# Another order of the items in three hand-written queue plans of an attention and expert kernel

## The chip, the cores and the metric

The kernel runs on one core of a Trainium2 chip. The metric is device time in microseconds of one launch. The engines are PE (matrix products; PEld is its loading of weights), DVE (elementwise work and reductions), ACT (activations and copies with a scale), POOL (elementwise work on SBUF alone) and SP (issues the DMAs). Each engine takes its own list of instructions in order; they wait for each other by semaphores.

## The reference, cut to what matters

Eight batches of 224 queries (512 wide) attend over 750 context rows with 8 heads of 64; then every token passes through all 8 experts of a gated feed-forward layer.

```python
x = x + tanh(g_xattn[0]) * xattn(layernorm(x), ctx, Wq, Wk, Wv, Wo, bo)
x = x + tanh(g_ffn[0]) * ffn(layernorm(x), gate_w, gate_b, rms_w, w1, b1, w2, b2)

def xattn(x, context, Wq, Wk, Wv, Wo, bo):
    q, k, v = heads(x @ Wq), heads(context @ Wk), heads(context @ Wv)
    attn = softmax(einsum("bihd,bjhd->bhij", q, k) * 64 ** -0.5)
    return einsum("bhij,bjhd->bihd", attn, v).reshape(B, N, 512) @ Wo + bo

def ffn(x, ...):
    h = gelu(einsum("nd,edh->neh", x, w1) + b1)
    y = einsum("neh,ehd->ned", h, w2) + b2
    return (y * norm_g[:, None, None]).sum(axis=1)
```

## The kernel before, in words

The kernel has an attention part (batch by batch) and an expert part (two halves of the tokens, 8 experts, four steps each). All products are made of float32r terms: an operand is split into a rounded high part and the rest, and three products (or two) are summed in PSUM. Therefore nearly every item on PE is drained twice: ACT writes the high part (function `hi`), then DVE the low part (`drain`).

The order of the attention part is not left to a scheduler. It is written out as three plans, each with one list for PE, ACT, DVE and POOL: `HEAD_PLAN` (what comes ahead of the first batch's heads), `BODY_PLAN` (one batch; the first batch leaves out its items of the batch before, the six middle batches are a loop) and `END_PLAN` (the last batch, with the first step of the experts woven in). Each engine walks its list, and `make` (PE), `hi` (ACT), `drain` and `special` (DVE) and `handle` (POOL) issue what an item needs of that engine, behind its semaphore waits. In an item, `>` means the next batch and `<` the batch before. The letters:

- `C` context columns split into parts (half, pair), `N` a piece of a weight matrix split, `X` the normalised queries transposed, `L` and `A` layer-norm statistics and their application, `Y` the same transposition for the expert part (drained by ACT alone).
- `K` keys (group, pair of heads, half: 12 matmuls), `Q` queries (group, pair: 12), `V` values (group, tile of 125 rows: 12).
- `S` scores of a head and half of the queries on PE (4 matmuls), their maximum on DVE, their exponential on ACT; `R` one over the row sum (DVE); `M` the scaling of the probabilities (half 0 on ACT, half 1 on POOL; in the last batch ACT does both from head 4 on).
- `T` two of six blocks of the probabilities transposed (head, third: 4 transpositions; the first third waits for both `M`), `P` the product with the values (6), `D` the sum of its terms (DVE, then POOL after each odd head), `O` the output projection (12, added to the residual by DVE).
- In the last plan `G`, `U`, `W`, `F`, `Z`, `B`, `H` are the experts' inputs, their split, the first weights, constants and the first step's seven products `H0` to `H6`.

What ties the order together is four PSUM banks. The items `X K Q V T O Y P B H` take them in turn in the order of PE's list (function `banks`), so each such item on PE first waits until the item four places earlier among these has been drained: by DVE's low part, for `Y` by ACT's copy:

```python
if before is not None:
    pe.wait_ge(lo_out[before[0]], number(before, b))
```

Scores have two places of their own: `S` waits for the exponential of the same half of the head before. The exponential of head h waits until PE has transposed all of head h-2, whose buffer it takes. `P` waits for the last `V` of its group, then for each third of its `T`. `K` of one half waits, per pair of context columns, for that pair's low part:

```python
for c in range(KC):
    pe.wait_ge(lo_out["C"], number(("C", db, half, c // 2), b))
```

SP's list (loads of context, x and weights, stores of both scratch tensors) is written separately and waits by the same semaphores.

## Time and profile before

| what | value |
|---|---|
| runs | 1819.58, 1821.06, 1828.24 us (median 1821.06) |
| span of the profiled execution | 1816.1 us, 31801 instructions, granted clock 1.000 |
| PE | 1794.9 us busy (99%), 9720 matmuls |
| PEld | 1615.8 us (89%) |
| DVE | 1330.5 us (73%) |
| ACT | 810.9 us (45%) |
| POOL | 1184.1 us (65%) |

The profiled execution's span is 5.0 us under the median of the runs. Busy time of PE is drawn from the start of each matmul to a modelled end, so neighbours overlap in the rows; the distance between two items is read from their starts. The attention part ends near 648 us; the first key projection begins at 8.03 us, the first batch near 35, the six middle batches lie between 106 and 573 us, 77.7 us each. The rest is the expert part.

### The profile page before, as it was taken

The page shows a single profiled execution, that of the slowest core. Times are in us where ns is not written, and L with a number is a line of the kernel's source. Part 1 is how long each engine was busy: PE and PEld are TensorE (multiplying, and loading weights), DVE is VectorE, ACT ScalarE, POOL GpSimd, SP SyncE. Part 2 cuts the span into 40 slices and gives each one's busy share as a digit, 9 for nine tenths or more (in the row PEclk, how much of TensorE's full clock was granted, in tenths as well). Part 3 has the DMA queues.
Part 4 walks back from the last instruction along what each step waited for, and adds up shares of the span by engine and source line. Part 5 has one row for each costly group of instructions (what it writes and reads, how often), then busy time and mean ns, then how long its engine had stood idle before and what let it go on. Part 6 is the DMA issues. An engine that isn't in the chain of part 4 may idle for free.

```text
span 1816.1 us, 31801 instructions
## 1 busy us (share of the span) xinstructions
PE 1794.9 (99%) x9720; PEld 1615.8 (89%) x9720; DVE 1330.5 (73%) x2308; ACT 810.9 (45%) x1574; POOL 1184.1 (65%) x900
## 2 busy tenths in 40 slices
...
GB/s 176 39 41 36 57 22 61 21 62 40 34 69 16 92 97 74 66 54 62 58 58 58 58 58 58 47 66 106 127 57 63 52 69 47 69 46 69 46 47 53
DMA packets 52057, 110.35 MB, mean 61 GB/s; under 512 B 13208, under 2 KB 25496, under 8 KB 52000
## 3 DMA queue, kind: packets, MB, share of 16 engines
...
q14 instruction: 27, 0.22, 0.0%
...
## 4 chain that ended last, share of the span: by engine, by line
PE 96%; DVE 1%; issue 1%; ACT 1%; DMA 0%; SPq 0%; POOL 0%; ACTq 0%; DVEq 0%
PE bank L781 33%; PE scores L754 28%; PE bank L625 19%; PE scores L696 5%; PE bank L706 4%; PE bank L718 4%; PE bank L632 1%; PE scores L839 0%; DVE h_sum L1051 0%; DMA ctx_raw<-in_ctx 0%; ACT hs L1318 0%; PE bank L754 0%; ACT probs L1190 0%; DVE xs L900 0%; ACT h_full L1317 0%
## 5 line engine op out<-in xcount | busy, mean ns | idle before, releaser
L781 PE MATMUL bank<-w2s,hs 128*128 128x512 f32 x2688 | 620.9, 389 | 1.3 <-DVE xres L1018 1.0
L781 PEld LDWEIGHTS bank<-w2s,hs 128*128 128x128 f32 x2688 | 504.4, 188 | 105.1 <-issue 1.5
L754 PE MATMUL scores<-xs,w1s 128*128 128x448 f32 x2646 | 549.5, 366 | 3.6 <-DVE h_sum L1051 3.5
L754 PEld LDWEIGHTS scores<-xs,w1s 128*128 128x128 f32 x2646 | 495.8, 188 | 48.7 <-DVE h_sum L1051 3.8
L1051 DVE TENSOR_TENSOR h_sum<-scores,h_sum 128x448 f32<-128x448 f32 x441 | 262.7, 619 | 183.3 <-PE scores L754 182.8
L1317 ACT ACTIVATE h_full<-h_sum,b1T 128x448 f32<-128x448 f32 x256 | 170.9, 668 | 303.1 <-DVE h_sum L1051 292.4
L1066 DVE TENSOR_TENSOR acc<-bank,acc 128x512 f32<-128x512 f32 x337 | 229.1, 686 | 71.5 <-PE bank L781 62.9
L900 DVE TENSOR_TENSOR hs<-h_full,hs 128x448 fp32r<-128x448 f32 x256 | 237.9, 930 | 52.2 <-ACT hs L1318 52.1
L1190 ACT ACTIVATE h_sum<-scores 128x448 f32<-128x448 f32 x63 | 34.3, 545 | 475.4 <-PE scores L754 475.4
L1391 POOL TENSOR_SCALAR probs<-probs,row_inv 112x750 f32<-112x750 f32 x60 | 130.6, 2176 | 100.1 <-DVE row_inv L989 100.1
L1493 POOL CAST w1s<-w_stage 128x768 fp32r<-128x768 f32 x64 | 69.0, 1078 | 168.5 <-PE scores L754 168.5
L1318 ACT ACTIVATE hs<-h_sum,b1T 128x448 fp32r<-128x448 f32 x256 | 167.7, 655 | 0.0
L1521 POOL TENSOR_TENSOR w2s<-w_stage,w2s 128x1024 fp32r<-128x1024 f32 x64 | 155.1, 2423 | 11.5 <-POOL w2s L1518 11.5
L1507 POOL TENSOR_TENSOR w1s<-w_stage,w1s 128x1024 fp32r<-128x1024 f32 x64 | 155.0, 2422 | 11.3 <-POOL w1s L1504 11.3
L625 PE MATMUL bank<-ctxT,wk 128*128 128x376 f32 (+1 forms) x768 | 147.0, 341 | 8.0 <-DVE ctxT L900 8.0
L625 PE MATMUL bank<-wv,ctxT 128*125 128x256 f32 x1152 | 152.1, 283 | 0.0
L625 PEld LDWEIGHTS bank<-wv,ctxT 128*125 128x125 f32 x1152 | 142.6, 186 | 1.0
L625 PEld LDWEIGHTS bank<-ctxT,wk 128*128 128x128 f32 x768 | 131.5, 191 | 10.4 <-issue 9.4
L1498 POOL TENSOR_TENSOR w1s<-w_stage,w1s 128x768 fp32r<-128x768 f32 x64 | 137.8, 2153 | 0.0
L1234 ACT ACTIVATE probs<-scores,neg_max 112x750 f32<-112x750 f32 x128 | 113.3, 886 | 32.1 <-DVE neg_max L983 20.8
L900 DVE TENSOR_TENSOR probsT<-bank,probsT 125x448 fp32r<-125x448 f32 x192 | 115.9, 618 | 12.7 <-ACT probsT L1190 11.1
L1190 ACT ACTIVATE probsT<-bank 125x448 fp32r<-125x448 f32 x192 | 100.0, 542 | 49.3 <-PE bank L706 49.0
(128 smaller groups left out, 2197.3 us busy)
## 6 DMA issues: line engine op xcount, KB each, us to landing
w_stage<-in_L_ffn_w SPq DMA_DIRECT2D x128, 512.0 KB, 3.5
...
xa<-in_x SPq DMA_DIRECT2D x16, 224.0 KB, 2.7
xres<-in_x SPq DMA_DIRECT2D x16, 224.0 KB, 2.7
x_scratch<-xres SPq DMA_DIRECT2D x16, 224.0 KB, 2.3
xt_scratch<-yT SPq DMA_DIRECT2D x16, 224.0 KB, 2.8
...
```

Source lines behind the costliest of these rows:

```text
L625: mm = pe.matmul(bank, s[i], m[j], start=first and n == 0, stop=last and n == total - 1)
L754: mm = pe.matmul(product_bank(g, name)[:, 0:TH], w1s[j % 2][:, s, W_OF[name], kc, :], xs[:, i, m, kc, :], start=n == 0, stop=n == 5)
L781: mm = pe.matmul(bank[:, :], hs[j % 2][:, s, ht, t * P:(t + 1) * P], w2s[j % 2][:, m, ht, :], start=n == 0, stop=n == 5)
L900: return dve.tensor_tensor(out, a_, b_.bitcast(F32), ALU.subtract)
L1051: dve.tensor_tensor(h_sum[:, q, :], product_bank(g, product)[:, 0:TH], h_sum[:, other, :], ALU.add).then_inc(sum_out, 1)
L1066: dve.tensor_tensor(home, ps[(3 * j + t) % RING][:, :], b2_sum[:, :] if first else home, ALU.add).then_inc(y_added, 1)
L1190: return act.activation(dst, src, ACT.Copy, scale=scale)
L1317: act.activation(h_full[:, q, :], src, ACT.Gelu, bias=bias)
L1318: act.activation(hs[j % 2][:, 0, ht, half * TH:(half + 1) * TH], src, ACT.Gelu, bias=bias).then_inc(h_act, 1)
L1498: pool.tensor_tensor(w[:, 1, 0:3], raw[:, 1:4], w[:, 0, 0:3].bitcast(F32), ALU.subtract).then_inc(w1_split, 1)
L1507: pool.tensor_tensor(w[:, 1, 3:7], raw[:, 4:8], w[:, 0, 3:7].bitcast(F32), ALU.subtract).then_inc(w1_split, 1)
L1521: pool.tensor_tensor(w[:, 1], w2_stage[:, :, :], w[:, 0].bitcast(F32), ALU.subtract).then_inc(w2_split, 1)
```

## The change

All three plans get new lists for all four engines. Each list holds the same items as before, in another order; the functions that issue them, the DMAs' list and all sizes stay. The lists of the last plan for ACT and POOL are left out here; in POOL's, `G0 G1 G2` now stand ahead of `W0.0`, and `G3` ahead of `W0.2`.

```diff
 HEAD_PLAN = {
     "pe": plan("""
-        K0.0.0 X0 X1 K0.1.0 Q0.0 Q0.1 K0.0.1 V0.0 V0.1 S0.0 S0.1 K0.1.1 S1.0 V0.2 V0.3 V0.4 S1.1 V0.5
+        K0.0.0 X0 X1 K0.1.0 Q0.0 Q0.1 K0.0.1 V0.0 V0.1 V0.2 S0.0 S0.1 K0.1.1 V0.3 S1.0 S1.1 V0.4 V0.5
     """),
     "act": plan("""
-        N0 C0.0 C0.1 N1 K0.0.0 C1.0 X0 N2 X1 C1.1 K0.1.0 Q0.0 Q0.1 K0.0.1 V0.0 S0.0 V0.1 K0.1.1 S0.1 V0.2 V0.3
-        S1.0 V0.4 S1.1 V0.5 M0.0
+        N0 C0.0 C0.1 N1 K0.0.0 C1.0 X0 X1 K0.1.0 C1.1 N2 Q0.0 Q0.1 K0.0.1 V0.0 V0.1 S0.0 V0.2 K0.1.1 S0.1 S1.0
+        V0.3 V0.4 M0.0 V0.5 S1.1
     """),
     "dve": plan("""
-        N0 C0.0 C0.1 L0.0 L0.1 A0.0 A0.1 K0.0.0 X0 N1 X1 C1.0 K0.1.0 C1.1 N2 Q0.0 K0.0.1 Q0.1 S0.0 R0.0 V0.0
-        S0.1 K0.1.1 V0.1 V0.2 S1.0 V0.3 R0.1 V0.4 S1.1 V0.5
+        N0 C0.0 L0.0 L0.1 C0.1 A0.0 A0.1 N1 K0.0.0 X0 X1 K0.1.0 C1.0 C1.1 N2 Q0.0 Q0.1 K0.0.1 S0.0 V0.0 S0.1
+        V0.1 V0.2 K0.1.1 R0.0 R0.1 S1.0 V0.3 V0.4 S1.1 V0.5
     """),
     "pool": plan("""
-        L0.0 L0.1 N3 N4 N5 N6 M0.1 N7
+        L0.0 L0.1 N3 N4 N5 M0.1 N6 N7
     """),
 }
 BODY_PLAN = {
     "pe": plan("""
-        K1.0.0 S2.0 S2.1 T0.0 T0.1 T0.2 O<0 K1.1.0 P0 S3.0 T1.0 T1.1 K1.0.1 S3.1 Q1.0 O<1 T1.2 V1.0 Y<0 K1.1.1
-        P1 T2.0 Y<1 S4.0 T2.1 S4.1 T2.2 V1.1 Q1.1 V1.2 V1.3 P2 S5.0 T3.0 S5.1 T3.1 T3.2 V1.4 P3 V1.5 V>0.0 S6.0
-        T4.0 T4.1 T4.2 V>0.1 S6.1 V>0.2 X>0 X>1 P4 S7.0 T5.0 T5.1 Q>0.0 K>0.0.0 T5.2 K>0.1.0 S7.1 K>0.0.1 V>0.3
-        P5 T6.0 V>0.4 S>0.0 S>0.1 T6.1 T6.2 Q>0.1 P6 T7.0 K>0.1.1 V>0.5 T7.1 T7.2 S>1.0 S>1.1 P7
+        K1.0.0 S2.0 T0.0 T0.1 S2.1 T0.2 K1.1.0 O<0 S3.0 P0 T1.0 K1.0.1 T1.1 S3.1 Q1.0 O<1 Y<0 T1.2 V1.0 K1.1.1
+        P1 Y<1 T2.0 S4.0 T2.1 S4.1 T2.2 V1.1 V1.2 Q1.1 S5.0 V1.3 P2 T3.0 T3.1 S5.1 T3.2 V1.4 V1.5 S6.0 P3
+        V>0.0 T4.0 T4.1 T4.2 V>0.1 S6.1 V>0.2 X>0 X>1 P4 T5.0 T5.1 S7.0 Q>0.0 K>0.0.0 K>0.1.0 T5.2 S7.1
+        K>0.0.1 V>0.3 P5 T6.0 S>0.0 S>0.1 V>0.4 T6.1 T6.2 Q>0.1 P6 T7.0 K>0.1.1 V>0.5 T7.1 S>1.0 T7.2 S>1.1 P7
     """),
     "act": plan("""
-        K1.0.0 T0.0 M1.0 T0.1 T0.2 S2.0 K1.1.0 P0 S2.1 T1.0 M2.0 T1.1 K1.0.1 Q1.0 S3.0 T1.2 V1.0 S3.1 Y<0 K1.1.1
-        P1 T2.0 Y<1 T2.1 T2.2 S4.0 M3.0 S4.1 V1.1 Q1.1 V1.2 V1.3 M4.0 P2 T3.0 T3.1 T3.2 P3 S5.0 V1.4 M5.0 V1.5
-        V>0.0 S5.1 T4.0 S6.0 V>0.1 T4.1 T4.2 X>0 V>0.2 X>1 M6.0 P4 T5.0 S6.1 T5.1 Q>0.0 T5.2 K>0.0.0 S7.0
-        K>0.1.0 S7.1 K>0.0.1 M7.0 P5 V>0.3 T6.0 V>0.4 T6.1 T6.2 S>0.0 Q>0.1 T7.0 M>0.0 P6 S>0.1 K>0.1.1 T7.1
-        V>0.5 T7.2 P7 S>1.0 S>1.1
+        K1.0.0 T0.0 T0.1 S2.0 T0.2 M1.0 K1.1.0 S2.1 P0 T1.0 T1.1 K1.0.1 Q1.0 S3.0 T1.2 Y<0 V1.0 M2.0 K1.1.1
+        S3.1 P1 T2.0 T2.1 Y<1 V1.1 S4.0 T2.2 S4.1 V1.2 M3.0 Q1.1 P2 V1.3 T3.0 T3.1 T3.2 S5.0 V1.4 V1.5 M4.0 P3
+        S5.1 V>0.0 M5.0 T4.0 S6.0 V>0.1 T4.1 T4.2 X>0 V>0.2 X>1 P4 T5.0 Q>0.0 S6.1 T5.1 K>0.0.0 K>0.1.0 T5.2
+        S7.0 S7.1 K>0.0.1 M6.0 P5 M7.0 V>0.3 T6.0 V>0.4 T6.1 T6.2 S>0.0 S>0.1 Q>0.1 T7.0 M>0.0 P6 K>0.1.1 T7.1
+        V>0.5 T7.2 S>1.0 P7 S>1.1
     """),
     "dve": plan("""
-        D<7 R1.0 R1.1 K1.0.0 T0.0 S2.0 T0.1 O<0 T0.2 S2.1 K1.1.0 D0 R2.0 S3.0 T1.0 L<1.0 T1.1 R2.1 S3.1 A<1.0
-        K1.0.1 Q1.0 O<1 L<1.1 T1.2 V1.0 A<1.1 K1.1.1 R3.0 D1 T2.0 S4.0 S4.1 R3.1 T2.1 T2.2 R4.0 V1.1 L>0.0 Q1.1
-        V1.2 V1.3 D2 T3.0 L>0.1 T3.1 T3.2 R4.1 S5.0 S5.1 R5.0 V1.4 D3 A>0.0 V1.5 V>0.0 S6.0 A>0.1 R5.1 T4.0
-        V>0.1 T4.1 R6.0 T4.2 X>0 V>0.2 X>1 S6.1 D4 T5.0 T5.1 Q>0.0 R6.1 T5.2 S7.0 K>0.0.0 S7.1 R7.0 K>0.1.0
-        K>0.0.1 D5 T6.0 R7.1 V>0.3 S>0.0 V>0.4 T6.1 T6.2 S>0.1 R>0.0 Q>0.1 T7.0 D6 K>0.1.1 T7.1 V>0.5 T7.2 R>0.1
-        S>1.0 S>1.1
+        R1.0 D<7 K1.0.0 R1.1 S2.0 T0.0 T0.1 S2.1 T0.2 K1.1.0 O<0 D0 T1.0 R2.0 R2.1 L<1.0 S3.0 A<1.0 K1.0.1
+        T1.1 Q1.0 O<1 L<1.1 A<1.1 T1.2 V1.0 R3.0 S3.1 K1.1.1 D1 T2.0 S4.0 R3.1 S4.1 T2.1 V1.1 R4.0 T2.2 L>0.0
+        R4.1 V1.2 Q1.1 V1.3 D2 T3.0 S5.0 T3.1 A>0.0 T3.2 L>0.1 V1.4 R5.0 S5.1 V1.5 D3 V>0.0 S6.0 R5.1 T4.0
+        A>0.1 T4.1 R6.0 V>0.1 T4.2 X>0 V>0.2 S6.1 X>1 T5.0 D4 S7.0 T5.1 Q>0.0 R6.1 K>0.0.0 S7.1 T5.2 K>0.1.0
+        R7.0 K>0.0.1 D5 S>0.0 V>0.3 R7.1 S>0.1 T6.0 V>0.4 T6.1 T6.2 R>0.0 Q>0.1 D6 T7.0 K>0.1.1 V>0.5 T7.1
+        T7.2 R>0.1 S>1.0 S>1.1
     """),
     "pool": plan("""
-        D<7 M1.1 L<1.0 L<1.1 M2.1 D1 M3.1 C>0.0 C>0.1 L>0.0 L>0.1 M4.1 D3 M5.1 C>1.0 C>1.1 M6.1 D5 M7.1 M>0.1
+        D<7 M1.1 L<1.0 L<1.1 M2.1 D1 M3.1 L>0.0 M4.1 C>0.0 C>0.1 L>0.1 M5.1 D3 C>1.0 C>1.1 M6.1 M7.1 D5 M>0.1
     """),
 }
 END_PLAN = {
     "pe": plan("""
-        K1.0.0 S2.0 T0.0 S2.1 T0.1 T0.2 O<0 O<1 P0 T1.0 Q1.0 Q1.1 S3.0 Y<0 K1.1.0 K1.0.1 T1.1 T1.2 K1.1.1 S3.1
-        P1 S4.0 T2.0 T2.1 V1.0 T2.2 V1.1 S4.1 V1.2 S5.0 P2 T3.0 T3.1 T3.2 S5.1 V1.3 V1.4 P3 S6.0 V1.5 S6.1 T4.0
-        Y<1 T4.1 T4.2 P4 S7.0 T5.0 T5.1 T5.2 S7.1 P5 B0 T6.0 T6.1 T6.2 H0 P6 H1 H2 T7.0 T7.1 T7.2 H3 P7 H4 H5 H6
-        O0 O1
+        K1.0.0 S2.0 T0.0 S2.1 T0.1 O<0 T0.2 O<1 P0 Q1.0 T1.0 S3.0 Q1.1 K1.1.0 Y<0 K1.0.1 T1.1 T1.2 K1.1.1 S3.1
+        P1 S4.0 T2.0 T2.1 S4.1 T2.2 V1.0 V1.1 S5.0 V1.2 S5.1 P2 T3.0 V1.3 T3.1 T3.2 V1.4 P3 S6.0 Y<1 V1.5 T4.0
+        S6.1 T4.1 T4.2 P4 T5.0 T5.1 T5.2 S7.0 S7.1 B0 P5 T6.0 T6.1 T6.2 P6 H0 H1 H2 T7.0 T7.1 T7.2 H3 P7 H4 H5
+        H6 O0 O1
     """),
...
     "dve": plan("""
-        R1.0 D<7 K1.0.0 T0.0 S2.0 S2.1 T0.1 T0.2 O<0 R1.1 O<1 L<1.0 L<1.1 T1.0 D0 R2.0 A<1.0 Q1.0 S3.0 Q1.1
-        K1.1.0 R2.1 A<1.1 K1.0.1 T1.1 T1.2 S3.1 R3.0 H0 K1.1.1 D1 T2.0 S4.0 T2.1 R3.1 R4.0 V1.0 S4.1 T2.2 V1.1
-        R4.1 V1.2 D2 S5.0 T3.0 T3.1 T3.2 S5.1 R5.0 S6.0 V1.3 V1.4 R5.1 D3 V1.5 T4.0 U0 T4.1 T4.2 S6.1 U1 R6.0
-        S7.0 R6.1 D4 T5.0 T5.1 T5.2 S7.1 D5 R7.0 B0 T6.0 T6.1 T6.2 U2 U3 U4 R7.1 D6 H1 H2 U5 T7.0 T7.1 T7.2 U6
-        H3 D7 H4 H5 H6 O0 O1 L1.0 L1.1 A1.0 A1.1
+        D<7 S2.0 R1.0 K1.0.0 T0.0 O<0 R1.1 S2.1 T0.1 T0.2 O<1 L<1.0 L<1.1 D0 A<1.0 T1.0 Q1.0 Q1.1 K1.1.0 A<1.1
+        R2.0 S3.0 T1.1 K1.0.1 R2.1 T1.2 S3.1 K1.1.1 D1 R3.0 T2.0 T2.1 R3.1 H0 S4.0 S4.1 V1.0 R4.0 R4.1 V1.1
+        T2.2 S5.0 V1.2 D2 S5.1 T3.0 T3.1 V1.3 T3.2 R5.0 D3 V1.4 R5.1 S6.0 T4.0 T4.1 T4.2 V1.5 S6.1 U0 U1 R6.0
+        R6.1 D4 T5.0 T5.1 S7.0 T5.2 B0 S7.1 R7.0 T6.0 D5 T6.1 T6.2 U2 U3 U4 R7.1 D6 H1 H2 U5 T7.0 T7.1 T7.2 U6
+        D7 H3 H4 H5 H6 O0 O1 L1.0 L1.1 A1.0 A1.1
     """),
...
```

## Rows read from the trace of the kernel before

**Rows 1.** Table of stretches: length, busy time (instructions) per engine, clock, DMA.

```profile
107.00:573.00 466.00, 465.58 (x3216) 447.69 (x3215) 382.33 (x817) 326.41 (x720) 217.40 (x181) 1.00 0.15 43
...
612.00:650.00 38.00, 33.85 (x179) 27.11 (x178) 34.04 (x59) 30.46 (x54) 28.09 (x24) 1.00 0.13 42
```

**Rows 2.** Timeline of PE, one middle batch: start, length, engine, line, operation.

```profile
363.16 1.38 PE L718 MATMUL bank<-probsT,values 125*128 125x448 f32 x6
364.62 0.66 PE L706 MATMUL bank<-ident,probs 112*125 112x112 f32 x4
...
366.54 0.92 PE L696 MATMUL scores<-keys,queries 128*112 128x376 f32 x4
...
367.65 1.66 PE L625 MATMUL bank<-wv,ctxT 128*125 128x256 f32 x12
369.15 1.49 PE L625 MATMUL bank<-xnT,wq 128*128 128x224 f32 x12
...
373.32 1.38 PE L718 MATMUL bank<-probsT,values 125*128 125x448 f32 x6
374.54 0.85 PE L696 MATMUL scores<-keys,queries 128*112 128x376 f32 x4
375.23 0.59 PE L706 MATMUL bank<-ident,probs 112*125 112x112 f32 x4
...
407.17 1.58 PE L625 MATMUL bank<-xnT,wq 128*128 128x224 f32 x12
...
412.31 1.59 PE L625 MATMUL bank<-wv,ctxT 128*125 128x256 f32 x12
```

**Rows 3.** Timeline of POOL in the same batch: the scaling M2.1.

```profile
362.29 2.18 POOL L1391 TENSOR_SCALAR probs<-probs,row_inv 112x750 f32<-112x750 f32 x1
```

**Rows 4.** Timeline of ACT in the same batch: T2.0, Y<1, T2.1, S4.0, M3.0, Q1.1, V1.3.

```profile
365.31 0.54 ACT L1190 ACTIVATE probsT<-bank 125x448 fp32r<-125x448 f32 x1 [0.38 <-PE bank L706]
365.75 0.54 ACT L1190 ACTIVATE yT<-bank 128x448 f32<-128x448 f32 x1
366.81 0.55 ACT L1190 ACTIVATE probsT<-bank 125x448 fp32r<-125x448 f32 x1 [0.52 <-PE bank L706]
...
368.36 0.88 ACT L1234 ACTIVATE probs<-scores,neg_max 112x750 f32<-112x750 f32 x1
...
369.22 0.92 ACT L1190 ACTIVATE probs<-probs,row_inv 112x750 f32<-112x750 f32 x1
...
371.15 1.44 ACT L1190 ACTIVATE queries<-bank 64x224 fp32r<-64x224 f32 x4
...
373.52 0.39 ACT L1190 ACTIVATE values<-bank 125x256 fp32r<-125x256 f32 x1 [0.52 <-PE bank L625]
```

**Rows 5.** Timeline of DVE in the same batch: Q1.1's low parts.

```profile
372.80 1.60 DVE L964 SCALAR_TENSOR_TENSOR queries<-bank,queries 64x224 fp32r<-64x224 f32 x4
```

**Rows 6.** Timeline of SP at the start: both loads of x issued.

```profile
2.32 0.95 SPq L456 DMA_DIRECT2D xa<-in_x  x2
```

**Rows 7.** DMA issues of the first 40 us: KB each, median us to landing.

```profile
xa<-in_x SPq DMA_DIRECT2D x2, 224.0 KB, 6.6
```

**Rows 8.** Timeline of DVE in the head: C0.1 and A0.0 (L0.0 and L0.1 between).

```profile
8.88 0.94 DVE L900 TENSOR_TENSOR ctxT<-ctx_raw,ctxT 128x752 fp32r<-128x752 f32 x1 [1.00 <-ACT ctxT L1190]
...
11.98 0.54 DVE L896 TENSOR_SCALAR xa<-xa,mean_var,rstd 112x512 f32<-112x512 f32 x1
```

**Rows 9.** Timeline of PE in the head: K0.0.0, K0.1.0, Q0.0.

```profile
8.03 4.10 PE L625 MATMUL bank<-ctxT,wk 128*128 128x376 f32 x12 [8.03 <-DVE ctxT L900]
...
13.95 2.31 PE L625 MATMUL bank<-ctxT,wk 128*128 128x376 f32 x12
17.13 1.12 PE L625 MATMUL bank<-xnT,wq 128*128 128x224 f32 x8 [0.86 <-DVE xnT L900]
```

**Rows 10.** Timelines of PE (P4) and DVE (U0) in the last batch.

```profile
618.80 1.21 PE L718 MATMUL bank<-probsT,values 125*128 125x448 f32 x4 [0.98 <-DVE probsT L900]
...
616.94 1.27 DVE L900 TENSOR_TENSOR xs<-x_raw,xs 128x896 fp32r<-128x896 f32 x1
```

12 lines of the change are left out of this document (6 added, 6 removed).

## The prediction

> **What bounds the kernel now.** I read the granted clock and span first (one core, 1816.1 us, clock 1.000), then the table of stretches, then who waits on PE, then the timeline of each engine in one middle batch. The table of stretches says that PE is the bound everywhere: in the six middle batches (107 to 573 us) it is busy 465.58 of 466.00 us, while DVE is busy 382.33 and ACT 326.41 [rows 1]. So an order can win only what PE still waits. Its visible idle time is 21.2 us in all, and 8.0 of that is the start, before the first key projection has its operands. The last batch is the one attention stage with much of it: 38.00 - 33.85 = 4.15 us between 612 and 650 [rows 1]. The two passes of experts after that are outside the three plans, and I move nothing there.
>
> The busy share of PE hides short waits, because a matmul that waits a tenth of a microsecond is simply drawn longer or later. I therefore read the distance from the start of one item to the start of the next. There are few such waits in a middle batch: P1 needs 364.62 - 363.16 = 1.46 us where P2 needs 374.54 - 373.32 = 1.22 [rows 2], because T2.0 behind it waits for the scaling M2.1, which POOL ends at 362.29 + 2.18 = 364.47 [rows 3]. T2.0 itself is then drawn 0.07 longer than its neighbours. That is 0.3 us per middle batch, nearly all that a better body order could give back.
>
> **The change, part by part.** Nothing is added or removed: the same items stand in each list, in another order. So the PE work stays, and each term is a wait that goes or comes. I went through the new lists queue by queue, put each item at the later of two times (its engine free, its input ready), and took durations and handovers from rows.
>
> *Body, gain.* O<1 keeps its place but Q1.0 is drained earlier on DVE (S3.1's maximum now comes after it), and PE reaches T2.0 0.3 us later behind Y<1. By the rows M2.1 ends about 0.5 us ahead of T2.0 then. The wait of 0.3 us goes: -0.3.
>
> *Body, first new wait: V1.1.* Four PSUM banks go round, so V1.1 takes the bank of Y<1 and waits for ACT's copy of it. PE now issues Y<1 before T2.0, but ACT's list has T2.0 T2.1 Y<1 V1.1. ACT can copy T2.1 only 366.81 - 366.54 = 0.27 us after PE starts S4.1; 0.55 for that copy and 0.54 for Y<1, less 0.10 of overlap, make 1.26 us [rows 2, 4]. The handover from ACT to PE isn't seen alone; it is not below 0, and the nearest row has 0.15 (M2.1's end to T2.0's start [rows 2, 3]). PE wants V1.1 367.65 - 366.54 = 1.11 us after S4.1's start [rows 2]. Cost 0.15 to 0.30; I take 0.25, nearer to the one handover that is seen.
>
> *Second: T3.1.* It takes the bank of Q1.1, which DVE must have finished. ACT now holds S4.0 T2.2 S4.1 V1.2 M3.0 behind V1.1, and Q1.1 behind them. From V1.1's end on PE: 0.20 until ACT starts, then 0.39 + 0.88 + 0.54 + 0.88 + 0.39 + 0.92 + 1.44 [rows 4], less about 0.45 of overlap between neighbours, is 5.2 us; DVE's four operations on Q1.1 add 1.60 [rows 5]: 6.8, and the handover, 0 to 0.15. PE reaches T3.1 after Q1.1, two V, P2, S5.0 (375.23 - 369.15 = 6.08 [rows 2]) and T3.0 (0.4): 6.5. Cost 0.30 to 0.45; I take 0.40. Before, ACT did T2.2, both exponentials and M3.0 while PE was still on V1.1, and PE did Q1.1 right behind it.
>
> *Third: V>0.5.* It takes the bank of Q>0.1. ACT now does S>0.1 ahead of Q>0.1. From the end of T6.2 on PE: 0.27 + 0.55 for T6.2, 0.88 + 0.88 for S>0.0 and S>0.1, 1.44 for Q>0.1, less 0.25 of overlap, then 1.60 on DVE: 5.4, and the handover. PE does Q>0.1 P6 T7.0 K>0.1.1 in 412.31 - 407.17 = 5.14 us [rows 2], the same four in both orders. Cost 0.3 to 0.5; I take 0.40.
>
> *Fourth and fifth:* X>1 behind DVE's T4.2 (DVE now does V>0.1 between T4.1 and T4.2) and Q>0.1 behind T6.0 (DVE has S>0.1 ahead of T6.0). By the same durations PE comes 0.05 to 0.25 and 0 to 0.15 us too early; I take 0.15 and 0.05, an estimate.
>
> Sum per middle batch: 0.25 + 0.40 + 0.40 + 0.15 + 0.05 - 0.30 = +0.95; with the lower ends 0.50, with the upper ones 1.35. Six batches: +5.7 (3.0 to 8.1). The first batch has no Y<, no O< and no M2.1 wait: the other four, +1.0 (0.65 to 1.35).
>
> *Moves that I cost at nothing.* T items between others instead of in runs: S4.1 and T2.2, each behind the other kind, take 367.65 - 366.54 = 1.11 together; an S behind a P takes 375.23 - 374.54 = 0.69 [rows 2] and a T within a run some 0.42 (an estimate), which is the same. POOL's M4.1, M5.1, M7.1 and M0.1 ahead of copies and D items: each ends 2 us or more before its T; what is put back, D3 (some 4 us with its two additions), must be ready when DVE reaches D4, and stays 0.7 us ahead; without that cover D4, and with it P5's bank, would be late by the difference. SP's list is unchanged. The stores and loads that wait for O<0 (now some 2 us later) are used 40 us later.
>
> *Head.* DVE now does L0.0 and L0.1 before C0.1. Both need the rows of x, issued from 2.32 us on [rows 6] with 6.6 us to landing [rows 7], so L0.0 starts at 8.9. The two take 11.98 - 8.88 - 0.94 = 2.2 us [rows 8], so C0.1 ends near 12.0 instead of 9.8. K0.0.0 has its first six matmuls from 8.03 and needs C0.1 for the other six: PE stands from about 10.2 to 12.1. Against that N1 is split earlier, so that Q0.0, which now starts at 17.13 after 0.86 us of waiting for X1 [rows 9], waits on X1 alone. Those twelve matmuls took 4.10 us, the next of the same shape 2.31 [rows 9]; 376 columns at the slower spacing (0.31) are the 1.2 GHz level, though the table prints the clock as 1.00 there. If the clock rises at 13.2 as now, K0.0.0 ends at 13.6, X1 is ready 0.5 later than now, and C1.0, C1.1 and N2, which DVE does after X1 now, hold nothing more: +0.5. If the rise comes later by the hole (1.9 us), X1 is 0.9 late, and K0.1.0, C1.0, C1.1, N2, Q0.0, Q0.1, K0.0.1 follow on DVE one behind the other: S0.0 is 1.2 late; if the rise starts afresh with the second half of K0.0.0, 2.1. I take +1.2. The Trainium skill (TensorE: Matmul & The Clock Gate, Part 1) says that the array is throttled by default and that activity releases it; by that a hole delays the rise, which speaks for the upper end, 2.1 instead of 1.2.
>
> *Last batch.* DVE no longer does U0 (1.27 us) between T4.0 and T4.1 [rows 10], which kept P4 waiting (the visible part is 0.98 us [rows 10]). But the new list puts V1.5 behind T4.2, P4 waits for V1.5 first, and P4 now follows T4.2 directly: 0.27 until ACT starts, T4.2's copy (0.55), and, as estimates from the sizes, 0.6 for its subtraction and 0.4 for V1.5's on DVE end some 1.9 us after PE is there. The wait changes its cause and hardly its size. H0 no longer fills PE between T6.2 and P6, so P6 waits 1.4 us for D5 and T6.2, and the same work follows: O0 starts as long after the batch's beginning as now. I take 0 (-2 to +2).
>
> Total: 5.7 + 1.0 + 1.2 + 0 = +7.9 us. The profiled execution goes from 1816.1 to 1824.0; the median of the runs is 5.0 above its span (1821.06), so 1829.0. By the bounds alone, 3.0 + 0.65 + 0.5 - 2 to 8.1 + 1.35 + 2.1 + 2: 1823.2 to 1834.6.
>
> **The rivals.**
>
> *The orders do what they say (not slower).* If the five waits don't show, say because a bank is given back 0.3 us earlier than I add up, the body gives -0.3 x 6, the head and the last batch's 4.15 us can give some 3: -5, 1816. It decides at spacings of 0.4 us, and the rows behind the second and third are sums of seven durations. For it: DVE has 18% of idle time in the body. Against it: ACT's and DVE's queues go in order, and those sums are longer than PE's.
>
> *DVE falls behind (clearly slower).* ACT's list has Q>0.0 S6.1 T5.1 and DVE's T5.1 Q>0.0, so DVE stands for 1.44 + 0.88 + 0.55 us after PE's Q>0.0. Following DVE from there (T5.1 Q>0.0 K>0.0.0 S7.1 T5.2 K>0.1.0) I get K>0.1.0's bank free 8.7 us after Q>0.0's end, and P5 wants it after 8.73. There is no margin; every further 0.1 us late costs 0.1 in each of seven batches. With 0.7 per batch: +4.9, 1834.
>
> *Nothing happens:* gains and waits cancel, 1821 +-1.
>
> *PE's own busy time shrinks.* The Trainium skill (Perfetto Trace Analysis, Identifying the Most-Contended Engine) holds that busy matmul time is a bad measure and that weight loads show the room. As a mechanism here: weight loads cover 447.69 of 466.00 us in the body [rows 1], so 18.3 us would be open to better neighbours: 1803. But the items with short loads (O, P) run at the spacing of their columns, which no order shortens.
>
> **How the numbers follow.** Forecast 0.55, orders work 0.20, DVE behind 0.14, nothing 0.09, shrinking 0.02. The forecast's own range is 1823.2 to 1834.6; to leave out no more than 2 in 10 I go to 1817 and 1836. What a measurement can tell from no change is about 0.5%, 9.1 us: slower than 1830.2 are the DVE case and about 0.22 of the forecast: 0.36. Faster than 1812 are the last case and a little of the second: 0.04. The rest, 0.60, is within.
>
> **What would show it.** Middle batches of 78.7 instead of 77.7 us; on PE a late start of V1.1, T3.1 and V>0.5 in each, less so of X>1; P1 back at 1.22; in the head a hole after six matmuls and a later first S; in the last batch P4 waiting for V1.5. I am wrong if the middle batches keep 77.7 or less, or if one new wait is over 0.6 us.

## The result and the profile after

The changed kernel takes 1842.61 us (median of 4 runs) against 1823.61 for the kernel before beside it (4 runs): ratio 1.0117, 95% interval 1.0092 to 1.0142. It is slower, as forecast, but outside the forecast range of 1817 to 1836. The span of the profiled execution is 1840.9 us, 24.8 more than before, three times the +7.9 of the forecast. Read from the starts of the items on PE, it is made of:

| stage | before | after | forecast | measured |
|---|---|---|---|---|
| head, to the first K1.0.0 | 35.26 | 37.65 | +1.2 | +2.39 |
| first batch | 71.12 | 73.70 | +1.0 | +2.58 |
| six middle batches | 466.35 | 479.86 | +5.7 | +13.51 |
| last batch, to the end of O1 | 75.39 | 77.89 | 0 | +2.50 |
| expert part | 1167.96 | 1171.81 | 0 | +3.85 |

A middle batch takes 80.0 us instead of 77.7 (forecast: 78.7). The table of stretches of the changed kernel (columns as in [rows 1]; six middle batches but for their edges, then 38 us of the last batch as in [rows 1]):

```profile
112.00:591.00 479.00, 475.52 (x3214) 447.54 (x3212) 380.19 (x816) 327.01 (x720) 216.76 (x181) 1.00 0.15 42
631.00:669.00 38.00, 33.48 (x180) 27.15 (x178) 32.06 (x55) 31.05 (x55) 26.53 (x25) 1.00 0.10 35
```

PE now visibly stands 3.5 us in the body, where it stood 0.4 [rows 1]; the other 10 us of the loss are drawn as longer or later matmuls. The waits on PE in the page of the changed kernel name what is new (engine, line, who was waited for: us in total, times, longest):

```profile
PE bank L625 <- DVE ctxT L900: 10.5, 3, 8.0
PE scores L754 <- DVE h_sum L1051: 5.5, 7, 2.0
PE bank L718 <- DVE keys L900: 2.1, 7, 0.4
PE bank L718 <- DVE values L900: 1.9, 1, 1.9
PE bank L718 <- DVE att_sum L1010: 1.3, 1, 1.3
PE bank L706 <- DVE queries L964: 1.0, 6, 0.3
...
PE bank L625 <- DVE keys L900: 0.4, 1, 0.4
```

The first is the head (8.0 at the start as before, then 2.1 and 0.4), the third P5 in seven batches, the fourth and fifth P4 and P6 of the last batch, the sixth T3.1 in six batches, the last V1.0 of the first batch. The second lies in the expert part, whose code is the same.

In a middle batch (the fifth of the eight) the items answering to [rows 2] are, on PE of the changed kernel, T3.0, T3.1, V>0.3, P5, T6.1 with T6.2, and Q>0.1:

```profile
387.31 0.59 PE L706 MATMUL bank<-ident,probs 112*125 112x112 f32 x4
388.05 0.69 PE L706 MATMUL bank<-ident,probs 112*125 112x112 f32 x4 [0.16 <-DVE queries L964]
...
413.39 1.58 PE L625 MATMUL bank<-wv,ctxT 128*125 128x256 f32 x12
415.26 1.49 PE L718 MATMUL bank<-probsT,values 125*128 125x448 f32 x6 [0.29 <-DVE keys L900]
...
419.80 1.02 PE L706 MATMUL bank<-ident,probs 112*125 112x112 f32 x8
420.91 1.60 PE L625 MATMUL bank<-xnT,wq 128*128 128x224 f32 x12
```

T3.1 starts 0.74 behind T3.0, where T items in a run follow after some 0.4: this is the forecast wait. P5 starts 1.87 behind V>0.3, whose matmuls need 1.42: this was only a rival in the prediction. In the kernel before, V>0.3, P5, and T6.1 with T6.2 (Q>0.1 follows at 407.17 [rows 2]):

```profile
400.50 1.58 PE L625 MATMUL bank<-wv,ctxT 128*125 128x256 f32 x12
401.92 1.39 PE L718 MATMUL bank<-probsT,values 125*128 125x448 f32 x6
...
406.37 1.02 PE L706 MATMUL bank<-ident,probs 112*125 112x112 f32 x8
```

There P5 follows 1.42 behind V>0.3, and Q>0.1 0.80 behind T6.1; in the changed kernel the latter is 1.11.

### The profile page after: what moved, and what is told of

It is laid out like the page before. It is cut to its first block, busy times and chain, and to the rows that moved or that the text cites. A ratio compares the mean times of both kernels' runs of the same rounds, so it can differ in the third digit from the quotient of the medians.

```text
span 1840.9 us, 31795 instructions
## 1 busy us (share of the span) xinstructions
PE 1810.7 (98%) x9720; PEld 1618.2 (88%) x9720; DVE 1331.3 (72%) x2308; ACT 812.0 (44%) x1574; POOL 1184.7 (64%) x900
## 3 DMA queue, kind: packets, MB, share of 16 engines
q1 hardware_dynamic: 52000, 109.64, 19.4%
## 4 chain that ended last, share of the span: by engine, by line
PE 75%; issue 10%; DVE 8%; ACT 4%; POOL 2%; DMA 0%; DVEq 0%; ACTq 0%; SPq 0%; POOLq 0%
PE bank L781 33%; PE scores L754 28%; PE bank L625 8%; PE bank L718 2%; PE bank L706 2%; DVE neg_max L983 2%; PE scores L696 2%; ACT probs L1234 1%; DVE probsT L900 1%; DVE queries L964 1%; DVE keys L900 1%; ACT queries L1190 1%; POOL probs L1391 1%; DVE h_sum L1051 1%; PE bank L632 0%
## 5 line engine op out<-in xcount | busy, mean ns | idle before, releaser
L983 DVE TENSOR_REDUCE neg_max<-scores 112x1 f32<-112x750 f32 x128 | 117.9, 927 | 2.4 <-PE scores L696 1.6
```

The costliest lines, as they stand in the source:

```text
L983: dve.tensor_reduce(neg_max[0:QT, i:i + 1], ps_scores[qt][0:QT, SCORES], AX.X, ALU.max, negate=True).then_inc(max_out, 1)
```

## The experiments

Item times below are distances between starts on PE. Lists are BODY_PLAN's unless another is named; of a list, only the items around a move are shown. A ratio is that to the kernel before, timed beside the run, with its 95% interval.

**Each plan alone.** Three kernels: the kernel before with one of the three new plans.

> The kernel before with the new HEAD_PLAN alone. Theory A (the loss of the head is the hole in PE behind the first six matmuls of K0.0.0, which DVE's later C0.1 causes, together with the slow first matmuls behind it): the first K1.0.0 starts 2.4 us later than before (35.3 to 37.7), the rest of the kernel keeps its distances, +2.4 us in all (about 1826). Rival B (by the prediction's working the hole costs 1.2; the other 1.2 us seen in the changed kernel belong to the body's lists, which take over K, V and S items in another order): +1.2 at the first K1.0.0, and the first batch keeps its 71.1 us.

> The kernel before with the new BODY_PLAN alone. Theory A (the loss is made of waits inside a batch): each middle batch takes 80.0 us instead of 77.7, the first batch 2.6 us more, so +16 us in all. Rival B (the lists of the three plans were found together, and part of the loss or gain lies at the seams to head and last batch): the middle batches still take 80.0, but the first or the last batch differ by over 1 us from what they take in the changed kernel (73.7 for the first). The prediction's working gives 78.7 for a middle batch and +6.7 in all.

> The kernel before with the new END_PLAN alone. Theory A (P4 behind V1.5 and P6 behind T6.2 in the last batch cost what they show, and nothing hides it): the last batch takes 2.5 us more than before, and the expert part keeps its length. Rival B (the prediction's working): P4's wait only changes its cause, the last batch keeps its length within 0.5. Rival C (the 3.8 us by which the expert part of the changed kernel is longer come from this plan's order of weights, loads and last items on POOL and DVE): the last batch +2.5 and the expert part +3.8, +6.3 in all.

These are the three parts of the diff ahead of the prediction. Measured: only_head 1822.88 us, ratio 1.0015 (1.0005 to 1.0025), first K1.0.0 at 36.89, first batch 71.0; only_body 1836.55, ratio 1.0087 (1.0070 to 1.0104), middle batches 80.0, first batch 73.73, last batch 75.64; only_end 1822.81, ratio 1.0013 (1.0003 to 1.0022), last batch 77.87. Each plan keeps its loss without the others, and the three ratios' excess over 1 (0.0015, 0.0087 and 0.0013) makes 0.0115 of the 0.0117 measured for all: the losses add and do not lie at the seams. The head's +1.6 lies between the two expectations. Of rival C for only_end: its profiled execution does have the expert part 3.7 longer, but only_body, with the old END_PLAN, has 2.5, and end_two_moves below, with the same list on POOL, has none. That difference has another cause (gate_later).

**ACT's T5.1 ahead of Q>0.0,** in the changed kernel:

```diff
-T5.0 Q>0.0 S6.1 T5.1 K>0.0.0
+T5.0 T5.1 Q>0.0 S6.1 K>0.0.0
```

> The changed kernel with one item moved in ACT's body list: T5.1 goes from behind S6.1 to ahead of Q>0.0, where DVE's list has it. Theory A (DVE stands 2.6 us for T5.1 behind Q>0.0 and S6.1 on ACT, falls behind, and gives the bank of K>0.1.0 back 0.55 us too late for P5, and by that Q>0.1 0.3 too late): P5 and Q>0.1 start without a wait, each middle batch takes about 79.2 instead of 80.0, -6 us in all. Rival B (DVE catches its idle time up before K>0.1.0, and P5 waits for ACT or for D items that share POOL): the middle batch stays within 0.2 of 80.0.

Measured: 1836.56 us against 1842.61 (ratios 1.0089, 1.0072 to 1.0106, and 1.0117); all six middle batches take 79.2, the number of theory A. On DVE, T5.1 and behind it Q>0.0 to K>0.1.0 in the changed kernel:

```profile
408.98 0.62 DVE L900 TENSOR_TENSOR probsT<-bank,probsT 125x448 fp32r<-125x448 f32 x1 [2.63 <-ACT probsT L1190]
409.52 1.59 DVE L964 SCALAR_TENSOR_TENSOR queries<-bank,queries 64x224 fp32r<-64x224 f32 x4
411.14 0.16 DVE L989 RECIPROCAL row_inv<-row_sum 112x1 f32<-112x1 f32 x1
411.34 1.11 DVE L900 TENSOR_TENSOR keys<-bank,keys 64x376 fp32r<-64x376 f32 x2
412.48 0.94 DVE L983 TENSOR_REDUCE neg_max<-scores 112x1 f32<-112x750 f32 x1
413.45 0.62 DVE L900 TENSOR_TENSOR probsT<-bank,probsT 125x448 fp32r<-125x448 f32 x1
414.10 1.11 DVE L900 TENSOR_TENSOR keys<-bank,keys 64x376 fp32r<-64x376 f32 x2
```

and with T5.1 moved, on PE, V>0.3, P5, T6.1 with T6.2, and Q>0.1:

```profile
410.21 1.58 PE L625 MATMUL bank<-wv,ctxT 128*125 128x256 f32 x12
411.62 1.39 PE L718 MATMUL bank<-probsT,values 125*128 125x448 f32 x6
...
416.06 1.02 PE L706 MATMUL bank<-ident,probs 112*125 112x112 f32 x8
417.17 1.60 PE L625 MATMUL bank<-xnT,wq 128*128 128x224 f32 x12
```

DVE stood 2.63 us for T5.1 and did 6 us of work behind it without a pause. Moved, P5 follows 1.41 behind V>0.3, without a wait, and the waits of the items ahead of it (S7.1, K>0.0.1) go too: 0.8 in all. But Q>0.1 still starts 1.11 behind T6.1, as in the changed kernel, so my guess that its 0.3 came from the late P5 was wrong: that 79.2 came out all the same was luck, since P5 and the items ahead of it gave 0.8 where I had 0.55. The last batch was 78.75 here, 0.9 longer, since PE's granted clock fell to 0.50 after its wait at P4 (row of this kernel's table of stretches):

```profile
636.00:638.00 2.00, 2.00 (x10) 1.99 (x9) 1.47 (x6) 1.76 (x5) 2.00 (x3) 0.50 0.00 0
```

**Three more moves on ACT, then three on DVE.** To the move above act_moves adds, on ACT, Q1.1 ahead of M3.0, S>0.1 behind Q>0.1 and Y<1 ahead of T2.0; act_dve_moves adds to these, on DVE:

```diff
-V1.0 R3.0 S3.1 K1.1.1 D1
+V1.0 R3.0 K1.1.1 S3.1 D1
-T4.1 R6.0 V>0.1 T4.2 X>0
+T4.1 R6.0 T4.2 V>0.1 X>0
-D5 S>0.0 V>0.3 R7.1 S>0.1 T6.0
+D5 T6.0 S>0.0 V>0.3 R7.1 S>0.1
```

> The changed kernel with four items moved in ACT's body list, each to where the wait that the prediction named would go: T5.1 ahead of Q>0.0 (alone it gave 0.8 per batch), Q1.1 ahead of M3.0 (T3.1), S>0.1 behind Q>0.1 (V>0.5), Y<1 ahead of T2.0 (V1.1). Theory A (each wait is the one ACT item in front): in a middle batch T3.1's wait of 0.4 and V1.1's of 0.2 go and V>0.5 loses its 0.1, so the batch takes 78.5 instead of the 79.2 with T5.1 alone. Rival B (the waits have a second cause close behind, DVE's queue, so that one move gives back little): not under 78.9.

> The same four moves on ACT and three on DVE: K1.1.1 ahead of S3.1 (bank of T2.1), T6.0 right behind D5 (bank of Q>0.1), V>0.1 behind T4.2 (bank of X>1). Theory A (Q>0.1's 0.32 is the maximum of S>0.1 ahead of T6.0 on DVE, the fifth term of the prediction at a wrong size, T2.1's 0.32 the maximum of S3.1 ahead of K1.1.1): both go and X>1's 0.2 too, the middle batch takes 77.7 or less, the same as before the change or 0.2 under it by the gain at M2.1, and the whole kernel is about 5 us over the kernel before, by its head and last batch. Rival B (Q>0.1 and T2.1 wait for something else, Q>0.1 for the late D5, T2.1 for A<1.1 that DVE does at half speed while POOL scales): 78.2 or more.

Measured: act_moves 1833.33 us, ratio 1.0063 (1.0039 to 1.0086), middle batches 78.95. T3.1's wait went (-0.40), but V1.4, three items later, came 0.27 later, and V1.1's 0.2 fell by 0.12 only. This is rival B's size. act_dve_moves 1852.56, ratio 1.0165 (1.0137 to 1.0192), middle batches 81.1 (one 83.1, in which the granted clock fell to 0.50 for some 3 us): the theory's 77.7 failed. The time lies within rival B's "78.2 or more", but not for its reason, since the moves did cause what they should (X>1's 0.17 and Q>0.1's 0.31 went, and T2.1 follows 0.76 behind S4.0 instead of 0.96) and made larger waits beside it. S4.1, which needs the exponential of S3.1, came 1.23 later, T2.2 behind it 0.48, and T6.1 0.88. On ACT of act_dve_moves, the exponential of S3.1, then P1 and Y<1; on DVE of the same, K1.1.1 and the maximum of S3.1:

```profile
385.88 0.89 ACT L1234 ACTIVATE probs<-scores,neg_max 112x750 f32<-112x750 f32 x1 [2.22 <-DVE neg_max L983]
...
386.88 0.35 ACT L1190 ACTIVATE att_tmp<-bank 64x224 f32<-64x224 f32 x1
387.25 0.54 ACT L1190 ACTIVATE yT<-bank 128x448 f32<-128x448 f32 x1
```

```profile
383.69 1.10 DVE L900 TENSOR_TENSOR keys<-bank,keys 64x374 fp32r<-64x374 f32 x2 [0.29 <-ACT keys L1190]
384.82 0.94 DVE L983 TENSOR_REDUCE neg_max<-scores 112x1 f32<-112x750 f32 x1
```

The maximum came 1.5 us later, and ACT stood for it 2.22 us with P1, Y<1, T2.0 and T2.1 queued behind; PE's S4.1 then stood 1.10 us for the exponential. A move on one in-order list lands on the other one.

**The head.** The kernel before with the new HEAD_PLAN and one move, then two, on DVE:

```diff
-N0 C0.0 L0.0 L0.1 C0.1 A0.0
+N0 C0.0 C0.1 L0.0 L0.1 A0.0
-X0 X1 K0.1.0 C1.0 C1.1 N2
+X0 X1 C1.0 K0.1.0 C1.1 N2
```

> The kernel before with the new HEAD_PLAN, and in it DVE's C0.1 again ahead of L0.0 and L0.1, nothing else. Theory A (hole and slow first matmuls behind it are the whole loss of the head): no hole behind the sixth matmul of K0.0.0, the faster spacing is there from about 13 us on as before, and the first K1.0.0 starts at 35.3 or earlier. Rival B (the other moves of the head cost too: V0.1, S1.0 and Q0.1 wait for drains that now come one behind the other on DVE): about 36.1.

> The kernel before with the new HEAD_PLAN, and on DVE C0.1 again ahead of L0.0 and C1.0 again ahead of K0.1.0. With C0.1 alone put back the hole in K0.0.0 went, but the first K1.0.0 stayed at 37.1, since K0.0.1 stood 0.75 us for the low parts of C1.0 and C1.1. Theory A (the step of the prediction that these hold nothing more was wrong, and they cost about 1 us of the head): K0.0.1 starts without its wait, S0.0 comes 0.7 to 1.0 us earlier behind Q0.0 than with C0.1 alone, the first K1.0.0 near 36.2. Rival B (what is left of the head's loss is the time at which the faster spacing comes, which differs from execution to execution): S0.0 comes as long behind Q0.0 as with C0.1 alone, 10.1 us.

Measured: with C0.1 alone (head_c01) the first K1.0.0 is at 37.11, with both (head_c1) at 35.51; the whole times don't tell either kernel from the one before (ratios 1.0002, 0.9986 to 1.0017, and 0.9997, 0.9985 to 1.0009). The hole (PE's pause) in K0.0.0, on PE of the changed kernel, then, on PE of head_c01, K0.0.0 in one piece and K0.0.1:

```profile
8.01 2.22 PE L625 MATMUL bank<-ctxT,wk 128*128 128x376 f32 x6 [8.01 <-DVE ctxT L900]
12.34 2.25 PE L625 MATMUL bank<-ctxT,wk 128*128 128x376 f32 x6 [2.12 <-DVE ctxT L900]
```

```profile
7.60 4.48 PE L625 MATMUL bank<-ctxT,wk 128*128 128x376 f32 x12 [7.60 <-DVE ctxT L900]
...
21.09 2.31 PE L625 MATMUL bank<-ctxT,wk 128*128 128x374 f32 x12 [0.59 <-DVE ctxT L900]
```

With the hole gone K0.0.1 still stood for C1.0, which DVE did behind K0.1.0, and DVE had waited 1.95 us for K0.1.0 with C1.0 ready. From Q0.0 to S0.0 it takes 10.11 in head_c01 and 9.10 in head_c1: theory A of head_c1 holds (1.0). In head_c01 neither theory A (35.3 or earlier) nor rival B (36.1) does. The other 0.6 between the two are the faster spacing: the granted clock rose at 12.2 us in head_c1 and at 17.1 in head_c01. From Q0.0 to the first K1.0.0, where the clock is up, it takes 18.1 in all ten profiled executions with the old list, 19.2 to 19.4 in the five with the new one, 19.4 in head_c01 and 18.4 in head_c1.

**The last batch.** Four kernels. end_two_moves (new END_PLAN; PE's H0 again between T6.2 and P6, DVE's V1.5 ahead of T4.0), end_h3 (new END_PLAN; DVE's H3 again ahead of D7), m61_pool (the kernel before; M6.1 on POOL behind D3), end_u6 (new END_PLAN; ACT's U6 again ahead of T7.0):

```diff
-T6.2 P6 H0 H1
+T6.2 H0 P6 H1
-T4.0 T4.1 T4.2 V1.5 S6.1
+V1.5 T4.0 T4.1 T4.2 S6.1
...
-U6 D7 H3 H4
+U6 H3 D7 H4
...
-T5.2 S7.0 M6.1 U2
+T5.2 S7.0 U2
-W0.2 D3 W0.3
+W0.2 D3 M6.1 W0.3
...
-H0 M7.0 M7.1 T7.0 U6 T7.1 T7.2
+H0 M7.0 M7.1 U6 T7.0 T7.1 T7.2
```

> The kernel before with the new END_PLAN, and in it H0 again between T6.2 and P6 on PE, and DVE's V1.5 ahead of T4.0 instead of behind T4.2. Theory A (the waits of P4 and P6 make most of the last batch's loss): P6's wait of 1.4 goes, P4's falls from 2.0 to about 1.5, and the last batch takes 76.0 instead of 77.9. Rival B (as in the prediction's working, filling PE there only moves the wait to the products H behind it, since the same work follows): 77.4 or more.

> The kernel before, with the scaling M6.1 of the last batch on POOL behind D3 instead of on ACT, the plans otherwise as before. Theory A (from 40 to 62 us of the last batch ACT stands idle for 0.4 us and sets the pace, so that 0.9 us less on ACT makes all behind it earlier): T7.0 and the end of the last batch come about 0.9 us earlier, 74.5 instead of 75.4 us. Rival B (PE's waits on DVE at P4, P5 and P6 set the pace, as the prediction had it): the last batch stays within 0.3 of 75.4 or gets longer, since POOL scales in 2.2 us.

> The kernel before with the new END_PLAN, and in it DVE's H3 again ahead of D7. Theory A (0.7 us of the last batch's loss is H6 on PE waiting for the bank of H3, which DVE drains only behind D7, and D7 waits for ACT's P7): the wait of 0.7 between H5 and H6 goes, the last batch takes 77.2 instead of 77.9; the rest, the 1.5 us that ACT stands idle longer, stays. Rival B (DVE's sums H5 and H6 behind set the end of the batch, whatever stands ahead of them): 77.8 or more.

> The kernel before with the new END_PLAN, and on ACT U6 again ahead of T7.0. In the new list ACT stands 0.84 us for T7.0 behind M7.1 and does U6 only then; in the list before U6 filled that wait. Theory A (at its end the last batch is paced by ACT and the chain M7.1, T7.2, H2, P7 on ACT, D7 on DVE and POOL, O0 on PE): T7.2, P7, D7 and O0 come 0.85 earlier, the last batch takes 77.0 instead of 77.9. Rival B (PE's waits at P4, P5 and P6 or DVE's sums set the end): within 0.3 of 77.9.

Measured, last batch: end_two_moves 77.92 against 77.87 for only_end. P4 started 1.34 earlier, but H0 in P6's place stood as long as P6 had (1.27 us in the rows), now itself behind D5 for the bank of P5, and T7.0 stood 1.09 us for ACT's scaling instead of 0.38, so that it starts 63.4 us into the batch as in only_end: rival B. end_h3 (79.0, one execution) is not clear: H6's 0.68 went, but O0 behind it came 0.77 later, since D7 was late then, and 1.07 were lost at P4 to the lower clock. m61_pool 78.62, 3.2 worse, as rival B allows, and theory A fails before it is tested: on PE the product H0 came at 633.31, when POOL ended the low half of its weights at 633.20 (in this execution the batch starts 2.1 us later than in the kernel before):

```profile
627.79 1.04 POOL L1504 CAST w1s<-w_stage 128x1024 fp32r<-128x1024 f32 x1
628.80 2.10 POOL L1473 TENSOR_TENSOR x_mix<-x_raw,x_mix 128x896 f32<-128x896 f32 x1
630.84 2.36 POOL L1507 TENSOR_TENSOR w1s<-w_stage,w1s 128x1024 fp32r<-128x1024 f32 x1
```

In the kernel before these weights end at 628.84 and H0 starts at 628.95 (the profile puts H0's wait down to DVE's copy for B0, which ends 0.12 ahead of the weights), and POOL stands 0.7 us in all from 605.7 to 629.9: POOL paces H0, and there is hardly room on it. In the batch H0 comes 2.2 later, the length of the scaling. Some of the 3.2 is again a clock of 0.50 for 3 us behind that pause. end_u6 77.09: theory A (0.8 of 0.85). On ACT of only_end, M7.0 with M7.1, T7.0 and U6, then, on ACT of end_u6, the same work without the pause:

```profile
634.05 1.72 ACT L1190 ACTIVATE probs<-probs,row_inv 112x750 f32<-112x750 f32 x2
636.61 0.54 ACT L1190 ACTIVATE probsT<-bank 125x448 fp32r<-125x448 f32 x1 [0.84 <-PE bank L706]
637.05 0.94 ACT L1190 ACTIVATE xs<-x_raw 128x896 fp32r<-128x896 f32 x1
```

```profile
634.50 1.72 ACT L1190 ACTIVATE probs<-probs,row_inv 112x750 f32<-112x750 f32 x2
636.12 0.94 ACT L1190 ACTIVATE xs<-x_raw 128x896 fp32r<-128x896 f32 x1
637.06 1.42 ACT L1190 ACTIVATE probsT<-bank 125x448 fp32r<-125x448 f32 x3
```

The whole times show little of this: ratios 1.0013 (0.9998 to 1.0028) for end_two_moves, 1.0020 (1.0009 to 1.0031) for m61_pool, 1.0000 (0.9989 to 1.0011) for end_u6, and a single 1821.92 us for end_h3.

**The gates' small operations behind the third sum,** in the kernel before (the call that issues them, moved from `step` into `sums`):

```diff
                 for name in {1: ("U2",), 2: ("C11",), 3: ("U3",), 4: ("C22", "V"), 5: ("C21",), 6: ("C12",)}.get(i, ()):
                     h_sums(g, name)
+                if i == 3 and g[2] == 3 and isinstance(g[1], int) and g[1] == NE - 1:
+                    gate(g[0], 2)
...
-                    if closing and j == 3 and i == 1:
-                        gate(p, 2)
```

> The kernel before with one move in DVE's expert part and nothing in the three plans: the six small operations on the gates (lines 1146 to 1151) of a pass's last step go from ahead of the third sum to behind it, where DVE stands 2.15 us for ACT anyway. Theory A (the 2.2 or 3.7 us by which the last 300 us are longer in some executions, of both kernels, come from two of these operations being held by a POOL operation that began just ahead of them, 1.04 for 0.17 us and 2.28 for 0.65): the expert part always has its shorter length, executions of the kernel before at 1820 to 1823 no longer occur, and the median is 1818, 2.5 us under that of before. Rival B (the difference comes from something else in the last 300 us, a load or the clock): median within 1 us of before, the same spread.

Measured: 1819.39 us (11 runs, 1818.5 to 1821.4) against 1820.10 (27 runs, 1817.7 to 1826.7), ratio 0.9994 (0.9985 to 1.0004). In the time theory A's number failed and rival B's held: the median is within 1 us of before, and four of the 11 runs lie at 1820 to 1822, where theory A wanted none. The traces do show theory A's mechanism. DVE, POOL and PE in the changed kernel:

```profile
1809.71 1.04 DVE L1148 TENSOR_SCALAR gate_small<-gate_small 128x7 f32<-128x7 f32 x1
1810.79 0.20 DVE L1149 RECIPROCAL gate_small<-gate_small 128x7 f32<-128x7 f32 x1
1811.02 2.28 DVE L1150 TENSOR_TENSOR gate_small<-gate_small 128x7 f32<-128x7 f32 x1
```

```profile
1809.68 1.04 POOL L1518 CAST w2s<-w_stage 128x1024 fp32r<-128x1024 f32 x1 [3.65 <-DMA w_stage<-in_L_ffn_w]
1810.90 2.37 POOL L1521 TENSOR_TENSOR w2s<-w_stage,w2s 128x1024 fp32r<-128x1024 f32 x1 [0.18 <-POOL w2s L1518]
```

```profile
1814.28 4.03 PE L754 MATMUL scores<-xs,w1s 128*128 128x448 f32 x12 [1.97 <-DVE h_sum L1051]
```

Both long operations end 0.03 behind the POOL operation that began ahead of them. In the kernel before POOL's cast begins 0.02 behind the first of the two, which takes 0.17; the second takes 0.65 and ends with that cast. Which starts first is decided by hundredths of a microsecond, between DVE's sum ahead of the gates and the transfer for which the cast waits. In nine of the fourteen profiled executions with the old place both operations are long, PE stands 1.9 to 2.0 us for the third sum, and the expert part is 2.0 to 3.9 us longer; in the other five, and in the three with the new place, PE has no such wait and the part takes 1167.8 to 1168.1. (In the new place one of the operations still takes 1.2 to 1.4 us, but nothing on PE waits for it.) Of the nine, seven lose 2.0 to 2.5. The changed kernel (3.9) and only_end (3.7) lose more, since there the granted clock also fell behind PE's wait; the row of the changed kernel's table of stretches:

```profile
1815.30:1818.60 3.30, 3.30 (x11) 2.85 (x10) 1.70 (x4) 1.96 (x4) 0.00 (x0) 0.50 0.01 2
```

**Versions meant to beat both.** best (three moves on the kernel before) and two_moves (without M6.1). The move in the body, on PE and on ACT:

```diff
-P1 T2.0 Y<1
+P1 Y<1 T2.0
```

> Three moves on the kernel before: the body's Y<1 ahead of T2.0 on PE and on ACT (the only wait that the new body gave back, at M2.1), the scaling M6.1 of the last batch on POOL, and the gates' small operations behind the third sum. Theory A (each gives what the theories say): middle batches of 77.4 instead of 77.7, a last batch of 74.5, the shorter expert part always: about 1815.5, 5 us under before. Rival B (Y<1 ahead of T2.0 only shifts the wait to V1.1, as in the changed kernel): middle batches of 77.7 or more, and only the other two gains, about 1817.

> Two moves on the kernel before: the body's Y<1 ahead of T2.0 on PE and on ACT (it gave 0.25 per middle batch in the run with three moves), and the gates' small operations behind the third sum; M6.1 stays on ACT, since on POOL it cost 3.2 us. Theory A: middle batches of 77.5, the last batch of 75.4 again, the shorter expert part always: 1.5 us under the kernel with the gates' move alone, about 1818, ratio 0.999. Rival B (the last batch's length was lost to its new start, not to M6.1): last batch still over 77, no gain.

Measured: best 1821.31, ratio 1.0005 (0.9995 to 1.0014): middle batches 77.47, but the last batch 79.39 by M6.1. two_moves 1818.00, ratio 0.9982 (0.9971 to 0.9993): middle batches 77.44, the shorter expert part, last batch 76.26 (with 0.81 as the clock between 625 and 630 us). It is faster than the kernel before by some 0.2% and than the changed one by 1.3%.

## Why the prediction was wrong in size

The direction and the way of reading (the distances on PE, each list walked in order) held: the loss is a row of small waits. Their sum was not. The step that failed is the list of waits in the body: +0.95 per middle batch was forecast and 2.25 measured, since the waits for a late bank at P5 (0.84) and at T2.1 (0.31) had no term and Q>0.1's was too small. Of the 16.9 us between forecast and measurement, 7.8 lie in the six middle batches, 1.6 in the first, 1.2 in the head, 2.5 in the last and 3.9 in the expert part.

- *The gain at M2.1* was right: P1 and T2.0 together need 0.37 less (forecast 0.3).
- *V1.1, T3.1 and X>1* were right: 0.20, 0.39 and 0.17 against 0.25, 0.40 and 0.15. *V>0.5* was 0.10 against 0.40. The prediction's own sum (5.4 on ACT and DVE, 5.14 on PE, a handover of up to 0.15) gives 0.2 to 0.4 and not 0.3 to 0.5; the rest fits Q>0.1, whose bank it takes, coming 0.32 late itself.
- *Q>0.1* was mis-sized, 0.32 against 0.05. The walk counted S>0.1's maximum ahead of T6.0 on DVE; V>0.3 and R7.1 stand there as well. act_dve_moves, with T6.0 moved, shows the wait gone.
- *T2.1* was missed: 0.31. It takes the bank of K1.1.1 and starts 0.06 behind the end of that item's low parts. On DVE, then on PE, of the changed kernel:

```profile
376.78 1.10 DVE L900 TENSOR_TENSOR keys<-bank,keys 64x374 fp32r<-64x374 f32 x2
```

```profile
377.94 0.69 PE L706 MATMUL bank<-ident,probs 112*125 112x112 f32 x4
```

  The prediction names S3.1's later place on DVE only as part of the gain; that its maximum (0.9 us) now stands ahead of K1.1.1 has no term. A<1.1 moved too, from behind V1.0 to right behind L<1.1: in all six middle batches DVE now stands 0.67 us for POOL's share of L<1.1 ahead of it and takes 1.12 us for it (row of A<1.1 in the last section), where it stood not at all and took 0.96. act_dve_moves, with S3.1 behind K1.1.1 and A<1.1 as in the changed kernel, ended T2.1's wait; whether A<1.1's old place would do so too, no run tells.
- *P5* is the largest miss: 0.84 with the items ahead of it, forecast 0. The rival "DVE falls behind" named the right items and "no margin", and should have been a term: its 1834 is the forecast's 1829 and 4.9 more, so the two were never alternatives. Its 8.7 us were measured as 9.2 (PE's Q>0.0 ends at 406.03, DVE's K>0.1.0 at 415.21). Two things are missing in it. Its list of DVE's items leaves out R6.1, between Q>0.0 and K>0.0.0 (0.16 in the seven rows above). And the lengths of the items it lists, 2.87 and 5.99 in these rows, make 8.86, so that 8.7 is reached only if neighbours overlap; but five of six handovers in the rows stand 0.03 to 0.04 apart and only one overlaps, by 0.08. act_t51_first settles that the wait starts at T5.1. As measured, the five waits of the forecast and its gain make 0.81, T2.1 and P5 another 1.15; the other 0.3 of the 2.25 lie in distances that differ by under 0.1 each, which no run separates.
- *First batch*: the same items, and V1.0 behind T1.2, which came 0.60 later there. O<1 and Y<0 are left out in this batch, so V1.0 takes the bank of K1.0.1 and waits for it (the line with 0.4 in the page above); in the old list it was the bank of T1.1. This had no term either.
- *Head*: two steps. The hole came as described, and with the matmuls behind it still slow, Q0.0 starts 1.2 us late (18.36 against 17.13 [rows 9]). From there to the first K1.0.0 another 1.2 were lost. The step that failed is the walk of DVE behind X1: in the case I took, K0.1.0, C1.0, C1.1 and what follows add 0.3 (X1 0.9 late, S0.0 1.2), and by head_c1 C1.0's place alone costs 1.0. Part of +2.39 is the execution: in ten profiled executions with the old list the first K1.0.0 starts at 34.95 to 37.50 (median 35.4), in five with the new one at 36.89 to 37.79 (median 37.65). What the hole costs apart from the time at which the clock rises stays open.
- *Last batch*: "the same work follows", so that O0 starts as long after the batch's beginning as before, failed: O0 comes 72.1 us after it (only_end) instead of 69.6. What I said of P4 and P6 was right, and end_two_moves confirms that they don't matter. But PE's 4.15 us of idle time [rows 1] hid that the last batch is not PE's from head 4 on: in the kernel before, ACT stands 0.5 us from 613.0 to 634.4, and POOL 0.7 from 605.7 to 629.9. With the new list (only_end) ACT ends M7.1 1.5 us later in the batch and then waits 0.84 for T7.0. end_u6 shows the second part; the 1.5 stay open: they stand in the trace as longer pauses of ACT up to P3 and at T6.0, and no run here separates these.
- *Expert part*: of +3.85 in the profiled execution, some 2.2 come and go in both kernels with the two held operations, and the rest with the clock behind PE's wait. I took the part as fixed, though the three runs of before already lay 8.7 us apart.

The range (1817 to 1836) was too narrow because the bounds of the five named waits were added up as if the list of waits were complete.
